# A long scan kernel whose two short stages are rewritten as two interleaved strands of neighbouring units

## What is computed

```python
# layer 0: a low-rank adapter per sequence (rank 8)
y = einsum('btd,bdr->btr', x, a1); y = einsum('btr,bdr->btd', y, bb1); y = gelu(y)
y = einsum('btd,bdr->btr', y, a2); x = einsum('btr,bdr->btd', y, bb2) + x
# layer 1: a state-space layer in both directions of time, then a gated MLP
def _ssm(h, in_w, xproj_w, dt_bias, A_log, Dskip, out_w):
    xs, z = split(h @ in_w); xs = silu(xs)
    proj = xs @ xproj_w
    dt = softplus(proj[..., :512] + dt_bias); Bm, Cm = the last 2 x 64 columns
    # hst = hst * exp(dt * A) + (dt * xs) * Bm ; y_t = <hst, Cm>, over 256 steps
    return (ys + xs * Dskip) * silu(z) @ out_w
h, gate = adaln(x); x = x + gate * (ssm_fwd(h) + flip(ssm_bwd(flip(h))))
h, gate = adaln(x); x = x + gate * (silu(h @ mlp_w1) * (h @ mlp_w2) @ mlp_w3)
# layers 2 and 3: a transformer block each, 16 heads, MLP of 1024
```

## Time and profile before

| | us |
|---|---|
| median of 3 runs | 8806.88 (8800.54 to 8809.34) |
| the profiled execution | 8806.76 |
| its span in the trace | 8805.0 |

### The profile page before, as it was taken

How to read it: one execution, slowest core, us unless ns; L and a number is a source line. 1 busy time by engine, 2 the same in 40 slices (tenths; PEclk the granted TensorE clock), 3 DMA queues, 4 the chain that set the end, 5 groups by cost and what they waited for, 6 DMA issues and landing times. The chain is left out here.

```text
span 8805.0 us, 233970 instructions
## 1 busy us (share of the span) xinstructions
PE 7370.3 (84%) x94400; PEld 3935.0 (45%) x94400; DVE 6316.8 (72%) x5549; ACT 5945.7 (68%) x8002; POOL 1345.0 (15%) x799
## 2 busy tenths in 40 slices
PE   7676757888888888888888888887779999989998
PEld 4333324444444444444444444443324444445454
DVE  1333339999999999999999999996224545455555
ACT  1333339999999999999999999994114444445554
POOL 0000002322222222223222222221000000000000
PEclk8777778999998998999889998998889999999999
DMA  4444442222222222222222222223320000000000
GB/s 141 108 92 105 92 105 67 66 66 66 66 65 66 66 66 66 66 66 66 66 66 65 66 66 66 66 66 113 118 105 5 8 8 8 5 27 10 11 10 6
DMA packets 621132, 541.65 MB, mean 62 GB/s; under 512 B 490225, under 2 KB 528753, under 8 KB 606449
## 3 DMA queue, kind: packets, MB, share of 16 engines
q1 hardware_dynamic: 620032, 526.35, 20.6%
HBM read 380.72 MB, written 145.49 MB: 60 GB/s over the span
## 5 line engine op out<-in xcount | busy, mean ns | idle before, releaser
L1086 DVE TENSOR_TENSOR_SCAN s_h<-s_decay,s_h 128x1040 f32<-128x1040 f32 x2048 | 4618.8, 2324 | 133.1 <-ACT s_decay L1010 129.0
L981 ACT COPY s_h<-s_pb 128x1024 f32<-128x1024 f32 x2048 | 2518.1, 1230 | 194.6 <-PE s_pb L912 169.5
L925 PE MATMUL s_py<-s_h,s_cz 128*32 128x128 f32 x32768 | 2516.3, 436 | 2.1 <-issue 1.3
L1010 ACT ACTIVATE s_decay<-s_pa 128x1024 f32<-128x1024 f32 x2048 | 2180.1, 1065 | 58.1 <-issue 47.4
L897 PE MATMUL s_pa<-s_dl,s_al 18*128 18x64 bf16 x32768 | 909.5, 198 | 667.7 <-ACT s_decay L1010 570.6
L925 PEld LDWEIGHTS s_py<-s_h,s_cz 128*32 128x32 f32 x32768 | 1057.4, 126 | 460.6 <-issue 5.9
L897 PEld LDWEIGHTS s_pa<-s_dl,s_al 18*128 18x128 bf16 x32768 | 661.9, 99 | 988.0 <-ACT s_decay L1010 912.4
L912 PEld LDWEIGHTS s_pb<-s_ul,s_bl 18*128 18x128 bf16 x16384 | 491.4, 97 | 1078.7 <-ACT s_h L981 859.1
L912 PE MATMUL s_pb<-s_ul,s_bl 18*128 18x128 bf16 x16384 | 866.3, 228 | 77.1 <-issue 60.5
L1053 POOL TENSOR_TENSOR s_h<-s_h,s_one 128x64 f32<-128x64 f32 x384 | 696.1, 1813 | 717.4 <-DVE s_h L1086 717.4
L1041 POOL TENSOR_TENSOR s_cz<-s_cl,s_one 128x128 f32<-128x128 f32 x256 | 330.5, 1291 | 2754.7 <-PE s_py L925 2742.5
(11 more groups left out here) (213 smaller groups left out, 6154.9 us busy)
## 6 DMA issues: line engine op xcount, KB each, us to landing
s_bl<-B SPq DMA_DIRECT2D x1024, 72.0 KB
s_ul<-U SPq DMA_DIRECT2D x1024, 72.0 KB
s_dl<-D SPq DMA_DIRECT2D x1024, 72.0 KB
s_al<-A SPq DMA_DIRECT2D x256, 144.0 KB
D<-p_dp SPq DMA_DIRECT2D x64, 384.0 KB, 6.5
U<-p_up SPq DMA_DIRECT2D x64, 384.0 KB, 5.3
B<-p_bz SPq DMA_DIRECT2D x144, 128.0 KB, 2.5
SZ<-p_sz SPq DMA_DIRECT2D x16, 1024.0 KB, 3.9
```

Of the source, the lines that this page charges most:

```text
L925: mm = pe.matmul(py[e % 2][QR * q:QR * q + QR, 0:P], cz[e % 2][:, l * P + QR * q:l * P + QR * q + QR], states, start=(l == 0), stop=(l == ...
L981: act.copy(out, pb[:].rearrange("p b t d -> p d b t")).then_inc(bu_done, 1)
L1010: act.activation(decay[(STEPS * e + 2 * z + j) % RING][:, :, 1:W], pa[j % 2][:], ACT.Exp).then_inc(exp_done, 1)
L1086: dve.tensor_tensor_scan(seg, decay[(STEPS * e + 2 * z + j) % RING][:].rearrange("p d w -> p (d w)"), seg, 0.0, ALU.mult, ALU.add).then_in ...
```

## The change

In `prepare`, each engine's queue is written out anew: pieces of the front part of unit i + 1 and the last steps of direction 1 of unit i - 1 stand between the steps of unit i. The banks are `g0` (4), `g1` (2) and a new `ga` (2) for the front part alone. z and the turned u go through `g1` in pieces of one bank (`to_z` by columns, `turn_u` by quarters q, with `first_u` and `first_rest_u` on ACT and DVE to match), xs has two tiles, and after a direction's u has been turned its first remainders come ahead of those of dt. The first unit's x is loaded ahead of the weights. In `finish_scan`, two rings of banks (`front`, 2 banks, and `back`, 5) serve two strands: projection and layer norm of unit i + 1 between the MLP products of unit i; x2 and mb have two tiles, the loads of y, sz and skip run a unit further ahead, and the weights are loaded behind the first unit's inputs. The instructions that compute are the same ones, but for the pieces. Functions that only got arguments or names (`low1`, `up1`, `softplus`, ...) are left out below, as are the removed lines of the old `unit` bodies, which the section above shows. The pieces are, in this order: tiles and banks, the loop over units, SP's unit, `to_z`, `turn_u` and TensorE's unit, ScalarE's unit, `first_rest_u` and VectorE's unit; then, of `finish_scan`, the two rings, TensorE's slot and VectorE's slot.

```diff
...
-        xs = sb("xs", [P, IC, N])
+        xs = [sb(f"xs{r}", [P, IC, N]) for r in range(2)]
...
-        g1 = c.enter_context(nc.psum_tensor("p_g1", [P, 4, 512], F32))
+        g1 = c.enter_context(nc.psum_tensor("p_g1", [P, 2, 512], F32))
+        ga = c.enter_context(nc.psum_tensor("p_ga", [P, 2, 512], F32))
...
+        def units(eng, body):
+            body(0, True, True)
+            with eng.Fori(1, UNITS - 2) as i:
+                body(i, True, True)
+            body(UNITS - 2, True, False)
+            body(UNITS - 1, False, False)
...
+                def unit(i, more, reads):
+                    if later(i):
+                        store_dt(i - 1, 1)
+                    store_gate(i, 0)
+                    if later(i):
+                        store_u(i - 1, 1)
+                    store_bc(i, 0)
+                    if more:
+                        front(i + 1)
+                    if reads:
+                        load(i + 2)
+                    store_dt(i, 0)
+                    store_gate(i, 1)
+                    store_u(i, 0)
+                    store_bc(i, 1)
+                units(sp, unit)
+                store_dt(UNITS - 1, 1)
+                store_u(UNITS - 1, 1)
...
+                def to_z(i, r, columns):
+                    n = 2 * i + r
+                    for m in columns:
+                        if m >= 2:
+                            wait(pe, s["sz_done"], IC * n + m - 1)
+                        elif r == 0:
+                            wait(pe, s["ures"], 4 * n - 1 + m)
+                        elif m == 0:
+                            wait(pe, s["cs_done"], 2 * n)
+                        else:
+                            wait(pe, s["bres_done"], n)
...
+                def turn_u(i, r, q):
+                    n = 2 * i + r
+                    if q == 0:
+                        wait(pe, s["u_done"], n + 1)
+                    if q >= 2:
+                        wait(pe, s["ures"], 4 * n + q - 1)
+                    elif r == 0:
+                        wait(pe, s["sz_done"], IC * (n + 1) + 3 + q)
+                    elif q == 0:
                         wait(pe, s["cs_done"], 2 * n + 2)
+                    else:
                         wait(pe, s["bres_done"], n + 1)
+                    for m in range(IC):
+                        mm = pe.transpose(g1[:, q % 2, m * P:(m + 1) * P], u[:, m, q * P:(q + 1) * P], ident[:])
+                    mm.then_inc(s["ut_mm"], 1)
...
+                def unit(i, more, reads):
                     wait(pe, s["h_done"], 4 * i + 4)
+                    to_xs(i, 0)
+                    if more:
+                        low1(i + 1)
+                    if later(i):
+                        turn_u(i - 1, 1, 0)
+                        turn_u(i - 1, 1, 1)
+                    if more:
+                        up1(i + 1)
+                    if later(i):
+                        turn_u(i - 1, 1, 2)
+                        turn_u(i - 1, 1, 3)
+                    to_dt(i, 0)
+                    to_z(i, 0, range(IC))
+                    if more:
+                        low2(i + 1)
+                    to_bc(i, 0)
                     wait(pe, s["hr_done"], i + 1)
+                    to_xs(i, 1)
+                    if more:
+                        up2(i + 1)
+                    to_z(i, 1, range(2))
+                    if more:
+                        mean(i + 1)
+                    to_z(i, 1, range(2, IC))
+                    if more:
+                        var(i + 1)
+                    turn_u(i, 0, 0)
+                    turn_u(i, 0, 1)
+                    to_dt(i, 1)
+                    turn_u(i, 0, 2)
+                    turn_u(i, 0, 3)
+                    to_bc(i, 1)
+                units(pe, unit)
+                for q in range(4):
+                    turn_u(UNITS - 1, 1, q)
...
+                def unit(i, more, reads):
+                    silu_xs(i, 0)
+                    if more:
+                        low(i + 1, 1)
+                    if later(i):
+                        for q in range(4):
+                            first_u(i - 1, 1, q)
+                        parts_dt(i - 1, 1)
+                    if more:
+                        gelu(i + 1)
+                    if later(i):
+                        second_u(i - 1, 1)
+                    silu_z(i, 0, range(IC))
+                    if more:
+                        low(i + 1, 2)
+                    softplus(i, 0)
+                    parts_b(i, 0)
+                    silu_xs(i, 1)
+                    parts_dt(i, 0)
+                    silu_z(i, 1, range(2))
+                    if more:
+                        square(i + 1)
+                    silu_z(i, 1, range(2, IC))
+                    if more:
+                        deviation(i + 1)
+                    for q in range(4):
+                        first_u(i, 0, q)
+                    second_u(i, 0)
+                    softplus(i, 1)
+                    parts_b(i, 1)
...
+                def first_rest_u(i, r):
+                    n = 2 * i + r
+                    wait(dve, s["dt_done"], n + 1)
+                    for q in range(4):
+                        wait(dve, s["up0"], 4 * n + q + 1)
+                        dve.tensor_tensor(sp_[:, q, :], g1[:, q % 2, :], up[:, 0, q, :], ALU.subtract).then_inc(s["ures"], 1)
...
+                def unit(i, more, reads):
+                    if later(i):
+                        first_rest_u(i - 1, 1)
+                        remainders_dt(i - 1, 1)
+                        second_rest_u(i - 1, 1)
+                    before_softplus(i, 0)
+                    skipped(i, 0)
+                    take_c(i, 0)
+                    to_dt(i, 0)
+                    remainders_b(i, 0)
+                    if more:
+                        residual(i + 1)
+                    remainders_dt(i, 0)
+                    if more:
+                        centre(i + 1)
+                    skipped(i, 1)
+                    if more:
+                        scale(i + 1)
+                    if reads:
+                        vectors(i + 2)
+                    first_rest_u(i, 0)
+                    before_softplus(i, 1)
+                    second_rest_u(i, 0)
+                    take_c(i, 1)
+                    to_dt(i, 1)
+                    remainders_b(i, 1)
...
+        front = Jobs([("po0", "v", 2), ("po1", "v", 2), ("mean", "v", 1), ("var", "a", 1)], 2)
+        back = Jobs([(f"{w}{m}", e, 1) for m in range(HC) for w, e in (("g", "a"), ("l", "v"))]
+                    + [("out0", "v", 2), ("out1", "v", 2)], 5, base=3)
...
+                def slot(i, e, more, gates, loads):
+                    wait(pe, s["h_done"], 4 * i + 4)
+                    gated(i, 0)
+                    if more:
+                        project(i + 1, 0)
+                    gated(i, 1)
+                    if more:
+                        project(i + 1, 1)
+                    gated(i, 2)
+                    if more:
+                        mean(i + 1, 1 - e)
+                    gated(i, 3)
+                    if more:
+                        var(i + 1)
+                    wait(pe, s["back_v"], back.taken(i, f"l{HC - 1}"))
                     for m in range(FC):
+                        output(i, m)
...
+                def slot(i, e, more, gates, loads):
+                    if more:
+                        vectors(i + 1, 1 - e)
+                    product(i, 0)
+                    if more:
+                        residual(i + 1, 1 - e, 0)
+                    product(i, 1)
+                    if more:
+                        residual(i + 1, 1 - e, 1)
+                    product(i, 2)
+                    if more:
+                        centre(i + 1, 1 - e)
+                    if gates:
+                        gate_y(i + 2, 0)
+                    product(i, 3)
+                    if gates:
+                        skip_y(i + 2, 0)
+                    if more:
+                        scale(i + 1, 1 - e, back.made(i, f"l{HC - 1}"))
+                    last_residual(i, e, 0)
+                    if gates:
+                        gate_y(i + 2, 1)
+                    last_residual(i, e, 1)
+                    if gates:
+                        skip_y(i + 2, 1)
...
```

More of the change, by code:

```diff
@@ new lines, in second_u @@
+                def second_u(i, r):
+                    n = 2 * i + r
+                    wait(act, s["ures"], 4 * n + 4)
+                    act.copy(up[:, 1], sp_[:]).then_inc(s["up1"], 1)
+                low(0, 1)
+                gelu(0)
+                low(0, 2)
+                square(0)
+                deviation(0)
+                def unit(i, more, reads):
[28 more added lines that the diff above has]
+                    parts_b(i, 1)
@@ L610, in _ @@
+                units(act, unit)
+                for q in range(4):
+                    first_u(UNITS - 1, 1, q)
+                parts_dt(UNITS - 1, 1)
```

(44 more changed lines are left out.)

730 lines of the change are left out of this document (372 added, 358 removed).

## The result

The changed kernel takes 8308.93 us (median of 4 runs, 8304.16 to 8313.26) against 8803.71 for the kernel before in the same session: a ratio of 0.9437, 95% interval 0.9424 to 0.945. The forecast was 8263 in a range of 8220 to 8350. The profiled execution took 8306.97 us, its span is 8305.2. A stage here runs from SP's first transfer for it to SP's first transfer for the next one; for the transformers, VectorE's first instruction counts.

A forecast was written before the change was run, and what follows sets the result against it. It saw `prepare` and `finish_scan` bound by chains between engines, none full, with TensorE idling and its clock dropping. Savings of 378 us in `prepare` and 166 in `finish_scan`, 544 together, took 8806.88 to 8263 us; range 8220 to 8350.

The forecast's parts named there:

- TensorE as the bound: Whole kernel: the main case, with TensorE's work setting the time, 8225 to 8300 us; chance 66%.
- The clock term: Unit of `prepare`: one idle slows TensorE's records behind it, 1.8 us per unit, bounds 0 and 4.
- The waits: Unit of `prepare`: TensorE's uncovered idle, 3.3 us for u of direction 1 and 4.1 for three small waits.
- the work of TensorE: Unit of `prepare`: TensorE's matmuls and transposes at 2.4 GHz, summed to 83.8 us.
- The scan and the transformers are not touched, and I carry them over unchanged: Scan and transformers: both stages keep their times, 4764.4 and 2222.3 us.
- The stores don't decide: Rival, `prepare`: stores of U hold up ScalarE, 8 to 10 us more per unit, 8340 us; chance 18%.
- The clock does not keep falling: Rival, `prepare`: small waits keep TensorE at 1.2 GHz for half of each unit, 8425 us; chance 7%.
- More is hidden: Rival, `prepare`: u's chain fully covered, no clock falls, 86 to 88 us per unit, 8215 us; chance 7%.
- Nothing gained: Rival, both changed stages: strands wait for each other at every step, periods stay, 8807 us; chance 1%.
- The slower rival: Rival, `prepare`: ScalarE's in-order wait for U's stores holds 68 us or more per unit; 8823 us at 70; chance 1%.
- The wait in the front strand: `prepare`, front part of the next unit: gelu or `low2` holding TensorE's queue, costed at nothing; would make the number wrong.
- The row of the table load: ScalarE's softplus in `prepare`: activation starts 1.29 us after its table load, no drain; the skill's rule would give 8274 us.

The follow-up runs named there:

- fin_only: The kernel before with only `finish_scan` changed, its `prepare` left as it was: 8635.7 us, ratio 0.9812.
- prep_only: The kernel before with only `prepare` changed, its `finish_scan` left as it was: 8470.3 us, ratio 0.9621.
- own_rest: The changed kernel with a separate tile for u's remainders, so direction 1's softplus need not wait for u's third part: 8272.3 us, ratio 0.9396.
- dt_first: The changed kernel with dt's parts and remainders put ahead of u's again for direction 1: 8323.2 us, ratio 0.9454.
- short_u: The changed kernel with a separate tile for u's remainders and u of direction 1 multiplied on VectorE instead of POOL: 8261.9 us, ratio 0.9388.

## Why the prediction was right, and where it was off

**Right in kind and size.** The measured 8308.9 lies in the range, but above the 8225 to 8300 that the prediction gave to TensorE as the bound, although TensorE is the bound: without the scan's 33 us it would be 8276. TensorE is the bound in both stages. `finish_scan`: 345.5 against 512.3 is 167 less, forecast 166; a slot is 37.8, forecast 38.3, its small waits being none at all. In `prepare` the start (106.4 for 105), the first front part (32.2 for 33.6), unit 0 (90.9 for 90) and the last unit with its tail (138.7 for 93 + 48) are within 3 us, and fin_only and prep_only show that the halves add up.

**The clock term was mis-sized.** "One such idle per unit: 1.8, bounds 0 and 4" measured 4.8. I had priced it from one group of records behind a 3.93 us idle and not asked which shorter groups stand in the slow stretch first: here two sets of transposes and a low-rank product paid 3.6 us before dt's product paid 1.2. The waits were 6.3 for 7.4, the work of TensorE 84.8 for 83.8. Over the six units up to the last, 575.7 us against 6 x 93.0 = 558: 17.7, nearly the stage's whole error. own_rest shows the two terms apart in its undisturbed units. Why the wait was 3.1, as forecast at 3.3: u's chain had the 2.3 us behind `up2` that I counted.

**"The scan and the transformers are not touched, and I carry them over unchanged"** is the step that failed: 33 us. The scan's own instructions are the same, but TensorE's code ahead of its loop is longer by more than a thousand instructions, since `prepare` now stands there four times instead of twice, and where the loop starts in it decides whether each of the 20 turns stops once or twice. Nothing in the trace of before says so.

**The rivals.** The stores don't decide: no row of ACT waits for them, and it takes twice the U to make it wait at all. The clock does not keep falling, not even behind a second wait (dt_first). "More is hidden" did not happen, but own_rest reaches 89.2 with one more tile, near its 86 to 88. "Nothing gained" is out with a unit of 95.9 instead of 146.73 us. The slower rival would have needed ACT to wait for U's stores, and nothing was near it. The wait in the front strand that I named as what would make the number wrong (gelu, `low2`) did not appear in the loop; own_rest and short_u find one of that kind, 0.20 and 1.06 us for the low-rank copy. The row of the table load was the better guide: from the load at 423.36 to the activation at 424.66 are 1.30 us, with no further drain as the Trainium skill, ScalarE: Activation LUTs, What ACT_TABLE_LOAD costs, would have it.

## What to carry to other kernels

Once an engine is nearly full, price an idle stretch by every record behind it that runs slow, not by one group: 3.08 us of waiting cost 7.9 here, and shortening it to 0.80 gave back 6.7 in the best units and 5.1 in the mean. Read more than one unit before you call a cost gone: the same short wait went unpunished in one unit and was followed by slow records in the next. Look at what the wait's chain shares: u's remainders and the softplus shared a tile, and a tile of its own was worth 37 us. And when a stage that the change does not touch gets longer, compare its gaps position by position in the loop, and try it with some unused instructions ahead of it, before looking for a cause in data or memory.

## What was not expected of the hardware

- A loop's place in TensorE's code is worth 40 us here: a second stop behind each of 19 jumps back (1.2 to 4.4 us in the changed kernel), at the same instruction with 0 and 256 instructions of padding, 16 instructions nearer to the start with 16, absent with 64 and 128.
- The jump itself stops TensorE for 3.1 to 3.9 us in every kernel (up to 4.8 in single turns), and ACT for about 3; VectorE's gaps at the first scan of a turn sum to 42 to 51 us in all of them. These are still there to be had.
- An idle of 3.08 us on TensorE was followed by records at 1.2 GHz that cost 4.8 us; a second idle of 3.26 us, 6 us behind the first, cost no more than itself. Idles of 0.7 to 1.1 us at the same place (own_rest, short_u) were followed by slow records in some units and by none in others.
- While POOL multiplies u (4.50 us from 429.06), VectorE's two subtractions for B's third part take 3.93 us together; with u on VectorE (short_u) they take 0.48.
